# TensorE waits for the end of its second weighing before projection Q1, in two of an item's four steps

## What is computed

```python
for i in range(6):
    x = attn_layer(shift_tokens(x), Wqkv[i], q_scale[i], k_scale[i], Wo[i]) + x
    x = ffn_layer(shift_tokens(x), ln_g[i], ln_b[i], W1[i], b1[i], W2[i], b2[i]) + x

def attn_layer(x, Wqkv, qs, ksc, Wo):          # 16 heads of 64, window 32
    q, k, v = split(x @ Wqkv)
    q = l2norm(q) * qs;  k = l2norm(k) * ksc;  rotary position factors on both
    sim = q @ k[own window and the one before].T * 8.0, masked
    return softmax(sim) @ v @ Wo

def ffn_layer(x, g, bln, W1, b1, W2, b2):      # hidden width 341
    a, gate = split(layernorm(x) * g + bln) @ W1 + b1
    return a * gelu(gate) @ W2 + b2
```

## Time and profile before

| | |
|---|---|
| three timed runs | 1710.77, 1713.35, 1713.54 us; median 1713.35 us |
| profiled execution | 1713.96 us |
| its span, first to last instruction | 1712.1 us |
| mean granted TensorE clock | 0.971 |
| busy share of the span | TensorE 93%, weight loads 75%, VectorE 85%, ScalarE 65%, GpSimd 62% |
| transformer, one item | about 66 us, of which TensorE is busy 61 to 66 |

### The profile page before, as it was taken

The page is one execution under the profiler, slowest core; times in us unless marked ns, Lnnn a source line. Parts: engine busy times, 40 slices in busy tenths (PEclk is TensorE's granted clock), DMA queues, the critical chain, the costliest instruction groups (busy, mean ns, idle before and its releaser), DMA issues.

```text
span 1712.1 us, 77709 instructions
## 1 busy us (share of the span) xinstructions
PE 1584.0 (93%) x33038; PEld 1281.2 (75%) x33039; DVE 1448.8 (85%) x3173; ACT 1116.5 (65%) x2014; POOL 1068.5 (62%) x1040
## 2 busy tenths in 40 slices
PE   4569999999999999999999999999999999999987
PEld 2247878777888777878777788777787778788774
DVE  8969989888889888989888889788889888888862
ACT  4346776666677666677666766666676676676663
POOL 3656767665667675666666577484676676566640
PEclk8579999999999999999999999999999999999999
DMA  2011110201111211111211111211011111111110
GB/s 87 31 45 49 41 50 25 77 25 49 44 37 37 71 31 46 34 50 38 59 35 48 42 37 41 57 42 51 25 54 40 50 50 36 37 48 40 38 46 14
DMA packets 41086, 75.09 MB, mean 44 GB/s; under 512 B 9472, under 2 KB 22568, under 8 KB 40744
## 3 DMA queue, kind: packets, MB, share of 16 engines
q1 hardware_dynamic: 40744, 70.12, 14.2%
HBM read 20.08 MB, written 2.10 MB: 13 GB/s over the span
## 4 chain that ended last, share of the span: by engine, by line
PE 70%; issue 9%; DVE 7%; ACT 4%; POOL 4%; ACTq 0%; DVEq 0%; POOLq 0%
PE bank L1360 8%; PE bank L1474 8%; PE bank L1329 8%; PE wide L1445 7%; PE bank L1405 7%; PE bank L1331 6%; PE bank L1330 6%; PE bank L1460 5%; PE bank L1538 4%; PE bank L1423 3%; PE bank L1523 2%; PE bank L1393 2%; POOL qk L857 2%; PE bank L1524 1%; PE bank L1525 1%
## 5 line engine op out<-in xcount | busy, mean ns | idle before, releaser
L865 POOL TENSOR_TENSOR qk<-qk,rnorm 128x512 f32<-128x512 f32 x384 | 401.1, 1045 | 347.4 <-DVE rnorm L1018 347.4
L857 POOL TENSOR_TENSOR qk<-qk,qk_sin 128x512 f32<-128x512 f32 x384 | 491.7, 1280 | 174.3 <-DVE qk_sin L979 174.3
L1181 ACT ACTIVATE squares<-bank 128x512 f32<-128x512 f32 x384 | 229.4, 597 | 150.1 <-DVE qk_sin L979 150.0
L1329 PE MATMUL bank<-w_hi,xs_hi 128*128 128x512 f32 x576 | 265.0, 460 | 22.0 <-issue 9.2
L989 DVE TENSOR_REDUCE norm<-squares 128x8 f32<-128x512 f32 x384 | 258.1, 677 | 30.6 <-ACT squares L1181 28.5
L972 DVE TENSOR_TENSOR qk<-bank,tables 128x512 f32<-128x512 f32 x384 | 261.3, 681 | 6.8 <-PE bank L1331 6.5
L979 DVE TENSOR_TENSOR qk_sin<-bank,tables 128x512 f32<-128x512 f32 x384 | 260.9, 679 | 0.6 <-POOL qk L857 0.6
L1360 PE MATMUL bank<-ident,qk 128*128 128x128 f32 x1536 | 227.3, 279 | 3.2 <-POOL qk L865 2.3
L1331 PE MATMUL bank<-w_hi,xs_lo 128*128 128x512 f32 x576 | 229.9, 399 | 0.0
L1330 PE MATMUL bank<-w_lo,xs_hi 128*128 128x512 f32 x576 | 228.4, 397 | 0.0
L1360 PEld LDWEIGHTS bank<-ident,qk 128*128 128x128 f32 x1536 | 181.8, 142 | 42.6 <-POOL qk L865 3.3
(11 more groups left out here) (181 smaller groups left out, 2728.5 us busy)
## 6 DMA issues: line engine op xcount, KB each, us to landing
v<-v SPq DMA_DIRECT2D x96, 390.0 KB, 3.5
v<-v SPq DMA_DIRECT2D x72, 130.0 KB, 3.7
w_raw<-in_L_ffn_Wqkv SPq DMA_DIRECT2D x36, 256.0 KB, 3.9
w_o_s<-in_L_ffn_Wo SPq DMA_DIRECT2D x6, 512.0 KB, 5.8
w_raw<-in_L_ffn_W SPq DMA_DIRECT2D x6, 341.0 KB, 4.1
mix_x_nat<-in_L_attn_x SPq DMA_DIRECT2D x4, 256.0 KB, 4.0
w_raw<-x_res_scratch SPq DMA_DIRECT2D x4, 256.0 KB, 3.3
out<-w_raw SPq DMA_DIRECT2D x4, 256.0 KB, 2.9
```

Source lines behind the costliest of these rows:

```text
L857: pool.tensor_tensor(qk[:, g % 2, c, :], qk[:, g % 2, c, :], qk_sin[:, (QK_CHUNKS * g + c) % SINES, :], ALU.add).then_inc(added[c], 1)
L865: pool.tensor_tensor(view, view, rnorm[:, g % 2, c * HPC:(c + 1) * HPC].unsqueeze(2) .to_broadcast([P, HPC, DH]), ALU.mult).then_inc(norme ...
L1329: pe.matmul(bank_of(c)[:], l_hi, w_hi[:, n, :], start=True, stop=False)
```

## The change

In steps t=1 and t=2, from step 9 on, TensorE waits before projection Q1 until its own second weighing of block step-3 has ended. In steps t=1 one mask product less is split (5 in place of 6).

```diff
             def mask_halves(step):
 
-                return (6, 6, 0, 0)[step % NBLK] if step >= FIRST_SPLIT else 0
+                return (6, 5, 0, 0)[step % NBLK] if step >= FIRST_SPLIT else 0
...
                 weigh(step - 3, 1)
+                if t in (1, 2) and step >= FIRST_SPLIT and live(step - 3):
+                    pe.wait_ge(weighed[1], 2 * (step - 2))
                 if step == BLOCKS + 4:
                     keep_busy(8)
                 if t == 0:
```

## The result

The changed kernel has a median of 1721.06 us over 22 runs (1711.17 to 1727.90), the kernel before 1711.81 us over 22 runs beside them (1707.54 to 1721.91). The ratio is 1.0045 [1.0031, 1.0058], so +7.7 us [5.3, 9.9]: slower, by more than the 0.2% that the forecast counts as a difference. The forecast was 1716.7 us (+3.3). The time lies in the forecast's range, on the side to which it leaned, but at more than twice the cost.

The account below looks back on a forecast made before the run. TensorE was taken to bound the kernel around the edit in t=1. Waits of t=1 at 3.3 us, t=2 at 0, mask and count at 0 gave +3.3 us, 1716.7 us (plus 0.19%); range 1709 to 1722 us.

Parts of the forecast that it names:

- The bound: Around the second weighing and Q1 in t=1, TensorE is the path, with no slack the chain shows.
- The price of one wait: Between second weighing and Q1: Q1's load moves from 0.79 to about 0.94 us, 0.15 us a wait, no queue refill.
- t=2 costs 0: The t=2 wait hides in the score's pause after product 92, at least 0.31 us; uncovered it would cost 3.3 us.
- The mask and the count: Mask of t=1: 0 us; two instructions fewer offset two added waits, so the pause stays at product 92.
- rival C: Item end: t=1 delay absorbed, 1713.4 us; or count not kept, later shorter pause, 2.9 us back, 1713.8 us; chance 0.16.
- The reading of the pauses: Score of t=2, after product 92: TensorE is out of instructions until a packet lands, late when queued behind transfers.
- The sum: Whole kernel: 3.3 us for t=1, 0 for t=2, 0 for mask and count, so +3.3 us.
- So all of it is paid: Wait before Q1 in t=1: 22 x 0.15 = 3.3 us, paid in full because what follows hangs on TensorE.
- A, both waits paid: The t=2 pause moves along: 6.6 us, 1720.0 us; or 0.36 us a t=1 wait, 7.9 us, 1721.3 us; chance 0.20.
- B, faster: Long score pauses shorten and avoid half clock, 1.42 us each; with five, 1709.5 us; chance 0.16.

Follow-up runs that it names:

- t=2 alone: Changed kernel with the real wait only in steps t=2 and an already satisfied one in t=1: 1.0013, 1715.46 us.
- satisfied waits: Changed kernel whose two added waits ask for a value reached a step earlier, same instruction count and order: 1.0001, 1713.17 us.
- t=1 alone: Changed kernel with the real wait only in steps t=1 and an already satisfied one in t=2: 1.0038, 1720.23 us.
- all four: Changed kernel with real waits in all four steps and one more mask product unsplit in t=0, keeping the count: 1.0023, 1722.41 us.
- first weighing: Changed kernel with already satisfied waits before Q1 and a real wait behind the first weighing of steps t=1: 1.0022, 1719.54 us.
- long wait in t=2: Changed kernel, in t=2 waiting before Q1 for VectorE's later reciprocal, in t=1 an already satisfied wait: 1.0005, 1718.04 us.
- long wait in t=1: Changed kernel, in t=1 waiting before Q1 for VectorE's later reciprocal, in t=2 an already satisfied wait: 1.0096, 1732.42 us.
- late loads: Kernel before, with SyncE issuing two groups of layer weights later, behind the next step's score or merging products: 0.9898, 1700.10 us.
- late loads with the change: Kernel before with the later weight issues plus the whole change, both waits and the mask: 0.9940, 1706.15 us.
- mask alone: Kernel before with only the t=1 mask's one split less and no waits, an item two instructions shorter: 1.0056, 1723.38 us.

## Why the prediction was right, and where it was too small

*The bound.* Right. TensorE is the path in step t=1, and what is put before Q1 there is paid in full in that step: 3.3 us in the trace for 22 x 0.15, and 20.5 us for 20.3 us of delay.

*The price of one wait.* Right: 0.15 us, worked out from two hand-overs of other engines, and measured at the first weighing too. It leaves no room for a refill of the queue.

*t=2 costs 0.* Right as to the mechanism: a wait that delays seven times as much is nearly all hidden in the same pause. The wait in t=2 alone measures 1.0013 [0.9991, 1.0036], which agrees but would not show it. What was said of the profile, pauses shorter by 0.15 us, isn't seen after the change (27.8 us in all against 23.8), and hidden in a scatter that is larger: five other kernels with the count kept have 27.2 (satisfied waits), 26.2 (t=1 alone), 24.8 (t=2 alone), 28.7 (all four) and 29.0 (first weighing).

*The mask and the count.* Right: 1.0001. That the count is kept turned out to be the costly half of the claim. An item two instructions shorter costs +0.56%, and two longer +1.01% with the waits' own cost in it, not the −2.9 us that rival C gave for a break that comes later. Its step, a later and so shorter pause, was wrong: as the break moves from 93 to 113 the pauses of t=2 are 34.5 us in all, counted on the weight loads, against 22.7 before.

*The reading of the pauses* as packets that come late: shown by the moving breaks, by the unbroken score behind a long wait, and by the later weights. The Trainium skill ("Runtime: NRT & Kernel Launch", section "Instruction fetch mechanics") has the crossing of a block as mostly hidden; the scores here lose 23.8 us to it.

*The sum.* The step that failed is "So all of it is paid", as a statement that nothing more is: 22 x 0.15 = 3.3 us, against 7.7 [5.3, 9.9] for the change and 6.5 [3.8, 9.2] for its t=1 half. The mechanism is right: in the stretch where the wait stands 3.3 us are paid. What the sum has at nothing is all that follows in the other steps, and there it is too small by 2.0 to 6.6 us.

What makes up these 2 to 6.6 us is **open**. No single part shows it: the instructions' positions measure 1.0001 [0.9979, 1.0023] and the wait of t=2 1.0013 [0.9991, 1.0036], intervals that leave room for a few us each. A doubling of each wait's delay is excluded (16.5 us for 20.3 with the long wait, 0.23% with all four). It could be longer pauses behind the delayed step, and one of 3.11 us with half clock behind it is in the profile; but the kernel with satisfied waits has as much idle time in its scores at no cost, so single profiles don't prove it. The table above puts the excess of the profiled execution over satisfied waits at 8.0 us in the stretches from t=2, which have 17.1 us at half clock against 6.8, and −3.1 in those from t=3. The batches also differ: the kernel before has medians of 1711.8 and 1712.9 us in the first two, where the change and its half measure 0.45% and 0.38%, and 1717.2 us in the third, where all four waits and the first-weighing wait measure 0.23% and 0.22%. Four kernels with a short real wait in t=1 have medians between 1719.5 and 1722.4 us, each on its chip; it is the kernel before that moves. The changed kernel itself wasn't run beside the before of 1717 us, so whether it would lose 0.2% there is not known.

Part of that difference is the granted clock, which is on record for each run. Runs of one and the same kernel are 1.2 to 1.7 us longer for each 0.001 by which their mean clock is lower. In the third batch the kernels with waits had 0.9746 and 0.9748 and the kernel before 0.9736; in the first t=1 alone had 0.9731 and the kernel before 0.9743. Set beside the kernel before at equal clock (one straight line of time against clock for the runs of each batch, an estimate; ± is a 95% interval), the costs of the short waits lie close together:

| kernel | us at equal clock |
|---|---|
| satisfied waits | 1.1 ± 2.1 |
| t=2 alone | 2.1 ± 2.1 |
| t=1 alone | 5.7 ± 2.1 |
| first weighing | 6.6 ± 2.0 |
| all four | 7.2 ± 2.0 |
| long wait in t=2 | 4.6 ± 2.5 |
| long wait in t=1 | 20.1 ± 3.2 |
| late loads | −7.5 ± 2.8 |
| late loads with the change | −7.4 ± 1.9 |

So the smaller ratios of the third batch are no sign of a smaller price; only the last two rows, from two chips, show no cost of the change. The long wait in t=1 costs its 20.3 us, of which a higher clock gave some 4 back; the long wait in t=2 isn't quite free; and more than half of what the late loads gain comes with the clock. Whether the waits change the clock or a run's clock differs by itself, these runs don't show.

*The rivals.* A, both waits paid: its total, 6.6 us, is nearer to the measurement than the forecast, but its mechanism, a pause that moves along, falls with the long wait in t=2; its other form, 0.36 us a wait in t=1, falls with the measured 0.15. B, faster: not seen; the time rose although the mean clock was 0.974 against 0.971. C, absorbed: falls with t=1 alone and with the long wait there.

*The range.* In part luck. The measured 1721.1 us lies in it only because its upper end was set by rival A's 1721.3 us, for a mechanism that isn't there.

## What to carry to other kernels

A wait of an engine for its own last result costs the hand-over (0.15 us here) in the step where it stands, all of it on the path and next to nothing in front of a stall that has another cause; that the whole program then lost 6.5 us for 3.3 stayed unexplained. So find for each stall what ends it before you price a wait ahead of it. Where a stall sits at the same instruction every time round the loop, count instructions: an edit that changes the length of the loop moves every packet end, and here two instructions an item were worth as much as the whole change (0.56%), so take it apart with a kernel that keeps the count and one that keeps the work. And when instruction packets come late, look at which large transfers leave just before them: issuing the weights behind the dense score instead of ahead of it gave 1.0%.

## What was not expected of the hardware

- A pause at a packet end doesn't go away as its place moves: with the waits and the old mask, where the t=2 break goes from product 91 to 71, it lasts 0.3 to 3.8 us, counted on the weight loads.
- Taking away one mask product an item cost 0.56% (mask alone), and 48 more instructions once, near the start, cost 0.62%.
- The total of such pauses scatters by several us without a change in time: 27.2 us with satisfied waits (1713.47 us) against 23.8 us before (1713.96 us).
- The same kernel before had medians of 1711.8 to 1717.3 us in the batches, 0.3% apart, more than this whole change was forecast to cost; an edit of this size needs ratios to runs on the same chip, and a look at the clock that both were granted.
